# Both phases of the z sums back to back at the end of TensorE's slot, in a graph attention kernel

## The reference

```
alpha = bn_relu(einsum('bchw,oc->bohw', x, wa))      # queries, 32 channels
sigma = bn_relu(einsum('bchw,oc->bohw', x, ws))      # keys, 32 channels
att  = softmax(where(adj, alpha_n . sigma_m, NEG))   # adj: the 8 neighbours
h_s  = einsum('bnm,bcm->bcn', att, xf)
Gc   = einsum('bcn,bdn->bcd', xf, xf)
catt = softmax(where(|c - d| == 1, Gc, NEG))
h_p  = einsum('bcd,bdn->bcn', catt, xf)
out  = (1 - gama) * x + gama * elu(h_s + h_p)
```

## Time and profile before

| what | us |
|---|---|
| median of 3 runs | 502.03 (498.39 to 506.97) |
| profiled execution, its own time | 500.11 |
| its span in the profile | 498.0 |
| TensorE busy | 461.8 (93%) |
| VectorE busy | 339.3 (68%) |
| ScalarE busy | 341.7 (69%) |
| GpSimd busy | 295.2 (59%) |

### The profile page before, as it was taken

The page is one execution under the profiler, slowest core; times in us unless marked ns, Lnnn a source line. Parts: engine busy times, 40 slices in busy tenths (PEclk is TensorE's granted clock), DMA queues, the critical chain, the costliest instruction groups (busy, mean ns, idle before and its releaser), DMA issues.

```text
span 498.0 us, 17890 instructions
## 1 busy us (share of the span) xinstructions
PE 461.8 (93%) x7172; PEld 350.4 (70%) x7172; DVE 339.3 (68%) x693; ACT 341.7 (69%) x980; POOL 295.2 (59%) x198
## 2 busy tenths in 40 slices
PE   1679999999999999999999999999999999999993
PEld 1346777768777786877767786877778687777783
DVE  6016676677767676766768677686767777686895
ACT  3336867677786777677776767787677776867571
POOL 8000566566756676567657656775666667665770
PEclk9998999999999999999999999999999999999985
DMA  7956667677776777676677767777677777644123
GB/s 224 264 137 166 190 206 241 194 217 225 224 226 211 236 209 239 206 238 210 206 228 215 243 203 226 222 228 224 217 218 231 219 224 226 197 156 143 65 107 128
DMA packets 55746, 102.01 MB, mean 205 GB/s; under 512 B 6256, under 2 KB 6640, under 8 KB 55664
## 3 DMA queue, kind: packets, MB, share of 16 engines
q1 hardware_dynamic: 55664, 100.88, 65.6%
HBM read 34.00 MB, written 33.55 MB: 136 GB/s over the span
## 4 chain that ended last, share of the span: by engine, by line
PE 84%; ACT 8%; DVE 3%; issue 3%; DMA 1%; SPq 0%; DVEq 0%; ACTq 0%
PE z L475 31%; PE gb L475 20%; PE xp L485 14%; PE score L475 12%; PE et L562 6%; ACT elu L302 2%; ACT key L263 2%; ACT upper L253 2%; PE gb L508 1%; ACT upper L267 1%; DVE elu L384 1%; DMA wt<-w_dram 1%; DVE z L379 1%; DVE probs_t L372 0%; DVE bn L424 0%
## 5 line engine op out<-in xcount | busy, mean ns | idle before, releaser
L228 POOL TENSOR_SCALAR elu<-elu,vec,mix 128x1024 f32<-128x1024 f32 x61 | 72.8, 1193 | 178.6 <-DVE elu L384 178.6
L475 PE MATMUL z<-probs_t,upper 64*128 64x128 f32 (+1 forms) x2304 | 173.2, 284 | 4.5 <-DVE probs_t L372 2.4
L475 PEld LDWEIGHTS z<-probs_t,upper 64*128 64x128 f32 x2304 | 155.2, 190 | 28.4 <-issue 24.1
L232 POOL TENSOR_TENSOR blend<-elu,blend 128x1024 f32<-128x1024 f32 x61 | 144.0, 2361 | 9.4 <-POOL elu L228 0.5
L302 ACT ACTIVATE elu<-z 128x512 f32<-128x512 f32 x128 | 69.7, 600 | 70.8 <-PE z L475 70.8
L384 DVE SCALAR_TENSOR_TENSOR elu<-elu,z 128x512 f32<-128x512 f32 x128 | 82.0, 682 | 35.4 <-ACT elu L302 35.4
L278 ACT ACTIVATE score<-score,neg_max 128x128 f32<-128x128 f32 x256 | 86.5, 338 | 25.1 <-DVE neg_max L355 25.1
L253 ACT ACTIVATE upper<-xp 128x512 f32<-128x512 f32 x128 | 76.8, 600 | 39.2 <-PE xp L485 39.2
L485 PE MATMUL xp<-const,x 128*128 128x128 f32 x512 | 87.2, 295 | 14.5 <-ACT upper L253 8.4
L379 DVE SCALAR_TENSOR_TENSOR z<-near,catt,z 128x512 f32<-128x512 f32 x128 | 90.4, 750 | 7.3 <-ACT z L293 6.6
L293 ACT ACTIVATE z<-x,catt 128x512 f32<-128x512 f32 x128 | 83.6, 695 | 2.4 <-DVE elu L384 2.4
(11 more groups left out here) (52 smaller groups left out, 244.1 us busy)
## 6 DMA issues: line engine op xcount, KB each, us to landing
x<-x_dram SPq DMA_DIRECT2D x64, 512.0 KB, 6.0
out_dram<-blend SPq DMA_DIRECT2D x61, 512.0 KB, 3.6
near<-x SPq DMA_DIRECT2D x128, 224.0 KB, 4.5
near<-x SPq DMA_DIRECT2D x128, 30.0 KB, 4.1
out_dram<-blend SPq DMA_DIRECT2D x6, 256.0 KB, 2.0
const<-constants_dram SPq DMA_DIRECT2D x1, 243.5 KB, 7.9
const<-constants_dram SPq DMA_DIRECT2D x1, 128.0 KB, 2.1
wt<-w_dram SPq DMA_DIRECT2D x1, 64.0 KB, 3.8
```

Source lines behind the costliest of these rows:

```text
L228: nc.gpsimd.tensor_scalar(elu[s % 2][:, :, :], elu[s % 2][:, :, :], vec[:, V_GAMA:V_GAMA + 1], mix[:, 1:2], ALU.mult, ALU.add).then_inc(ga ...
L232: nc.gpsimd.tensor_tensor(blend[s % BLENDS][:, :, :], elu[s % 2][:, :, :], blend[s % BLENDS][:, :, :], ALU.add).then_inc(blend_done, 1)
L475: return nc.tensor.matmul(o, l, r, start=start, stop=stop, skip_group_check=True, **kw)
```

## The change

In TensorE's slot the first phase of the z sums moves behind the second transposes of x and the transposes of the probabilities, and the second phase follows it directly. In a slot with `q == 0`, `gram_band(b, 2)` moves behind the probabilities' transposes and `gram_band(b, 3)` behind both phases, so that it stands directly in front of `shift_gram(b)`. In a slot with `q == 2`, `project_odd` now stands in front of both phases. The instructions themselves are the same ones, and the other engines' orders are unchanged.

```
                     gram_band(b, 1)
                 if q == 3 and 0 < b + 1 < B:
                     project_even(b + 1)
-                if real(t - 2):
-                    z_sums(t - 2, 0)
-                if own:
-                    gram_band(b, 2)
                 if b + 1 < B:
                     transpose_x(b + 1, q, 1)
                 if real(t - 1):
                     transpose_probs(t - 1)
                 if own:
-                    gram_band(b, 3)
+                    gram_band(b, 2)
                 if q == 2 and 0 < b + 1 < B:
                     project_odd(b + 1)
                 if real(t - 2):
+                    z_sums(t - 2, 0)
                     z_sums(t - 2, 1)
+                if own:
+                    gram_band(b, 3)
                 if q == 1 and 0 < b + 1 < B:
                     project_query(b + 1)
```

More of the change, by code:

```diff
@@ L605, in _ @@
                     project_even(b + 1)
[L606 to L609, removed]
                 if b + 1 < B:
```

## The result

The changed kernel takes 554.29 us (median of 4, 551.64 to 556.90) where the kernel before takes 504.50 beside it (median of 4): a ratio of 1.108, 95% interval 1.097 to 1.120. The sign was forecast, the size was not: 534 was predicted, and 549 was the end of the range. The profiled execution took 554.69 us with a span of 552.8, so 54.8 us more than the span of before.

What follows compares the result with a forecast made beforehand. TensorE's queue was taken to set the pace. Stall 17.1, touching z phases 7.2 and clock 8 gave 32.3 us on the profiled 500.11, 532.4; the median lies 1.9 higher, so 534 us, range 517 to 549.

Steps and rivals of the forecast that it cites:

- The sign: Whole kernel: slower by over 2%, given a chance of 0.91.
- The bound, and what moves at no cost: TensorE's queue sets the pace; earlier transposes of x and probabilities cost nought, at most 0.2 us per slot.
- rival E: VectorE's 36.1 us wait for the probabilities' transposes is on the path; its loss makes the kernel faster, 488 us; chance 0.02.
- Term 1: In front of `shift_gram`: uncovered wait for `gram_side` plus late `normalise`, 1.14 us per image, 17.1 us, bounds 13 to 21.
- Term 2: Second z phase waits uncovered for the first's end: 0.12 us per slot, 7.2 us in all, bounds 2.4 to 12.
- Term 3: Clock falls behind the new stalls at `shift_gram`: 1.6 us each in a third of 15 images, 8 us, bounds 0 to 24.
- The end of the run: Last slots: VectorE sets the pace; the new order may save or cost half a microsecond.
- Rival C: The clock falls in every image behind the stall, 24 us for the clock, 550 us in all; chance 0.15.

Runs made afterwards that it cites:

- e_repaired: Kernel before, with the transposes early as in the change and whatever the slot has between the z phases; 494.39 us against 501.21, ratio 0.987.
- e_even_late: Kernel before, with `project_even` moved behind the first z phase in slots with q = 3; 490.90 us against 502.67, ratio 0.977.
- e_gram_front: Changed kernel with parts 2 and 3 of the channel products in front of both z phases; 508.98 us against 502.67 for the kernel before, ratio 1.011.
- e_fill: Changed kernel plus four unused 512-column matmuls between part 3 of the channel products and `shift_gram`, images 1 to 15; 524.91 us, ratio 1.042 to the kernel before.
- e_gap_q1: Kernel before, with four chained one-column matmuls as a gap in front of `project_query`, slots with q = 1, 14 images; 511.97 us, ratio 1.018.
- e_gap_q0: Kernel before, with four chained one-column matmuls as a gap in front of `shift_gram`, slots with q = 0, 15 images; 527.39 us, ratio 1.050.
- e_gram_back: Kernel before, with only part 3 of the channel products moved behind the second z phase, directly in front of `shift_gram`; 536.02 us, ratio 1.064.
- e_apart_q0: Changed kernel with part 2 of the channel products between the z phases where q = 0; 550.88 us against 500.20 for the kernel before, ratio 1.093.
- e_apart_q1: Changed kernel with the first z phase back ahead of the second transposes in slots with q = 1; median 549.76 us, from 538.55 to 558.09.

## Why the prediction was wrong in size

**The bound, and what moves at no cost: right.** TensorE's queue sets the pace. The earlier copy of the probabilities brought nothing, and rival E was wrong as argued. The early transposes are free (e_repaired, 0.12 us an image more than e_even_late, all of it the touching pair).

**Term 1: right.** 0.87 us idle, and 0.19 for the late `normalise`: part 3 to `shift_gram` 1.52 us, forecast 1.53. That slot 0 of the old trace already ran the new order made this term exact.

**Term 2: right.** 0.12 us for each slot, read from a receiver on another engine; with it an image without a fall costs 1.64 us more, forecast 1.14 + 4 x 0.12 = 1.62. e_gram_front gives 6.3 us for the whole term, forecast 7.2. The estimate of 10 us from the Trainium skill (TensorE: Matmul & The Clock Gate, Single matmul latency) was too high for this wait: 0.12 us measured against its 0.166. Both terms together are 24.3 us in the forecast and 22 in e_fill.

**Term 3: the step that failed, as "5 x 1.6 = 8 us".** The mechanism was named, and e_fill shows it: fill the stall and the clock stays. Both factors were too small. I took a third of the images, by one counterexample at 92 us and a count of two; nine of 13 fell. And I took a fall to last as in slot 1, 3.4 us and 1.6 us of time; most last about 7 us, and 3.0 us is the mean. 9 x 3.0 = 27 instead of 8, before the end of the run.

The share had little under it: one stall with a fall behind it, at 36 us (the other fall that the prediction counts, at 472 us, lies behind the last image), and one without, at 92 us. The words "amid dense work" gave the second a reason that its own neighbourhood does not bear out. It stands in a slot with q = 0 like the new stalls, with part 3 of the channel products and three z matmuls in front, and the rest of the z phase, `shift_gram`, transposes and scores behind:

```profile
91.44 0.65 PE L475 MATMUL gb<-upper 128*32 128x33 f32 x40
92.03 0.43 PE L475 MATMUL z<-probs_t,upper 64*128 64x64 f32 x3
93.54 1.10 PE L475 MATMUL z<-probs_t,upper 64*128 64x128 f32 x15 [1.08 <-issue]
94.58 0.38 PE L475 MATMUL gb<-gram,const 128*128 128x1 f32 x2
```

So it is not like the forgiven gaps of e_gap_q1, which stand in front of matmuls of 512 columns. It is one more stall at the end of such a slot that kept the clock, as four of 13 did in the changed kernel and nine of 14 gaps in e_gap_q0. What it showed is that a fall is not certain; one case for and one against could not give the share.

**The end of the run: not priced.** I left the slots after the last image to VectorE, give or take half a microsecond. They take 6.0 us more. With the stall filled they take 34.5 (e_fill, 488.54 to 523.0) against 32.8 before, so most of it is clock: it falls at about 517 us behind the last image's stall and stays low for some 20 us. The stall is not the whole reason. The kernel before is at half clock there too, from 473 us for nearly 4 us and again from 487 for 11, and in other kernels with the same stall this part takes 35.2 us (e_gram_back), 39.6 (e_apart_q0) and 32.0 (e_apart_q1), one execution each. Why the clock stays low for so long there is not shown.

**The range.** Rival C, 550, was the nearest and had 0.15. Its 24 us, the upper bound of term 3, assumed one short fall for each image; the true course was fewer, longer falls and a slow end. That rival C came near in its number is luck. The range ended below it and left the cause with the largest unknown too little room.

**What stays open.** Why some images with the same stall keep the clock (in the profiled execution the one at 331 us and the four from 394 to 485), why a fall lasts 3.5, 7 or 10 us, whether the length of a gap, the kind of work around it or both decide on a fall, and whether touching phases add to the loss. The changed kernel has a clock of 0.918 to 0.931 and e_gram_back one of 0.940 to 0.946, and the changed kernel loses 10 us more than e_gram_back and e_gram_front do together (49.8 against 33.4 + 6.3); the two runs that should have told why are too scattered.

## What to carry to other kernels

Before a block is moved in a hand-written order, look at what it covers for the wait that follows: here 1.3 us of matmuls hid an engine's answer of 0.9 us. A short stall of TensorE has two prices, its own length and that of the clock afterwards; take the second from a stall in the same neighbourhood, but one stall gives neither how often the clock falls nor for how long, so let the range cover a longer fall behind every stall. Where a wait on another engine is known, put independent matmuls in front of it; that alone made the kernel 2.3% faster (1.6 to 3.0).

## What was not expected of the hardware

The clock fell to 1.2 GHz within three microseconds of a stall of 0.87 us between stretches of full work, in nine images of 13, and stayed there for 3.5 to 10 us in the steady part and for 20 us at the end. A stall of 0.33 us in the same place, behind two matmuls of 512 columns, had no such effect in any of 14 images, nor a gap of 0.94 us between z sums and matmuls of 512 columns. By itself: the Trainium skill (TensorE: Matmul & The Clock Gate, A second HAM failure mode: psum-queue depth-cycling) says of another kernel that frequent micro-idles between groups of matmuls made the clock swing between its two levels; the trace of the changed kernel agrees, at 0.918 over the span against 0.983 with the stalls filled (e_fill). And unneeded work can pay: four unused matmuls in each of 15 images made the changed kernel 29 us faster.
